# Chunkwise memory update: VectorE's work of a step in another order, with the pending result and its statistics moved into two waits

## The reference, cut to what matters

```python
def step(M, chunk):
    ...                                     # eta, alpha: means of sigmoids of the chunk
    outputs = einsum('bci,boi->bco', chunk, M)
    k_mean = (chunk / norm(chunk)).mean(axis=1)
    v_target = value_gen(outputs).mean(axis=1)   # value_gen(y) = silu(y @ w1.T) @ w2.T + y
    err = v_target - einsum('boi,bi->bo', M, k_mean)
    M_new = alpha * M + eta * err[:, :, None] * k_mean[:, None, :]
    M_new = gate * M_new + (1 - gate) * M
    M_norm = sqrt(sum(M_new * M_new))
    return M_new * minimum(30.0 / (M_norm + 1e-6), 1.0), outputs
M_final, outs = scan(step, M0, chunks)
x = x + value_gen(outs)
```

## Time and profile before

| | |
|---|---|
| median of 3 runs | 1940.58 us |
| lowest, highest run | 1935.58, 1942.81 us |
| profiled execution: span (no other time is listed for it) | 1946.8 us |
| TensorE busy over the span | 1855.2 us, 95% |
| VectorE busy over the span | 1348.6 us, 69% |
| ScalarE, GpSimd busy | 1179.6 us (61%), 416.6 us (21%) |
| the 16 memory steps | from about 66 to 228 us of the span |

### The profile page before, as it was taken

How to read it: one execution, slowest core, us unless ns; L and a number is a source line. 1 busy time by engine, 2 the same in 40 slices (tenths; PEclk the granted TensorE clock), 3 DMA queues, 4 the chain that set the end, 5 groups by cost and what they waited for, 6 DMA issues and landing times. The chain is left out here.

```text
span 1946.8 us, 51759 instructions
## 1 busy us (share of the span) xinstructions
PE 1855.2 (95%) x19836; PEld 1437.6 (74%) x19836; DVE 1348.6 (69%) x2724; ACT 1179.6 (61%) x2371; POOL 416.6 (21%) x497
## 2 busy tenths in 40 slices
PE   6998899999999888999999999999998999999998
PEld 5677789999999654465555555565545789999997
DVE  6555678544445877899999999999944877444445
ACT  5211354554545544799889988989895644445443
POOL 1121100455553333000000000000000002555541
PEclk9999999999999999999999999999999999999999
DMA  7000121222225665312122111111005211222228
GB/s 303 1 1 0 39 76 29 66 79 74 80 71 170 153 180 150 89 42 54 44 55 49 42 41 41 41 42 41 3 3 200 100 36 35 78 76 79 74 65 265
DMA packets 86539, 149.13 MB, mean 77 GB/s; under 512 B 35620, under 2 KB 69284, under 8 KB 80612
## 3 DMA queue, kind: packets, MB, share of 16 engines
q1 hardware_dynamic: 68428, 103.24, 17.6%
q0 software_dynamic: 17856, 42.60, 7.9%
q10 hardware_dynamic: 24, 0.02, 0.0%
HBM read 96.68 MB, written 48.76 MB: 75 GB/s over the span
## 5 line engine op out<-in xcount | busy, mean ns | idle before, releaser
L2201 ACT ACTIVATE att_scores_pt<-att_scores_psE 128x512 f32<-128x512 f32 x1024 | 598.1, 597 | 68.6 <-PE att_scores_psE L1705 26.3
L1720 DVE TENSOR_REDUCE att_mx<-att_scores_psS 128x1 f32<-128x1024 f32 x472 | 578.1, 1225 | 49.8 <-PE att_scores_psS L1705 18.5
L1705 PE MATMUL att_scores_psE<-att_qs,att_ks 99*32 99x512 bf16 x4096 | 438.1, 382 | 3.9 <-DVE att_scores_psO L2231 3.1
L2303 PE MATMUL att_scores_psO<-att_scores_pt,att_va 128*17 128x256 f32 x4096 | 330.5, 379 | 2.9 <-ACT att_scores_osb L2206 1.3
L1705 PE MATMUL att_scores_psS<-att_ks,att_qs 96*32 96x512 bf16 x3776 | 308.8, 380 | 0.1
L1705 PEld LDWEIGHTS att_scores_psE<-att_qs,att_ks 99*32 99x32 bf16 x4096 | 137.0, 95 | 102.8 <-ACT att_scores_pt L2201 8.8
L2303 PEld LDWEIGHTS att_scores_psO<-att_scores_pt,att_va 128*17 128x17 f32 x4096 | 132.5, 98 | 102.3 <-issue 13.2
L658 DVE TENSOR_TENSOR moe_hidT_rest<-moe_ps,moe_hidT_high 128x384 fp32r<-128x384 f32 x142 | 79.2, 558 | 184.9 <-ACT moe_hidT_high L377 172.2
L865 PE MATMUL moe_ps<-W_rest,moe_srcT_high 128*128 (+2 forms) x824 | 200.3, 324 | 0.0
L283 POOL DMA_INDIRECT expert_rows<-work,moe_slots_i x142 | 140.0, 986 | 218.8 <-issue 108.1
L1705 PEld LDWEIGHTS att_scores_psS<-att_ks,att_qs 96*32 96x32 bf16 x3776 | 127.1, 98 | 77.0 <-issue 1.3
(11 more groups left out here) (327 smaller groups left out, 3146.3 us busy)
## 6 DMA issues: line engine op xcount, KB each, us to landing
W_gate_up<-in_gate_up_dram SPq DMA_DIRECT2D x2, 6346.0 KB, 21.8
work<-expert_rows SPq DMA_DIRECT2D x12, 1024.0 KB, 7.9
query_key_parts<-att_qkv_parts SPq DMA_DIRECT2D x64, 192.0 KB, 2.8
normalised_rows<-work SPq DMA_DIRECT2D x64, 128.0 KB, 1.9
att_qs<-query_key_parts SPq DMA_DIRECT2D x16, 384.0 KB, 4.4
att_ks<-query_key_parts SPq DMA_DIRECT2D x16, 384.0 KB, 4.5
W_down<-in_down_a_dram SPq DMA_DIRECT2D x2, 2304.0 KB, 28.1
work<-normalised_rows SPq DMA_DIRECT2D x36, 128.0 KB, 2.1
```

What stands on the lines that cost most here:

```text
L1705: last = nc.tensor.matmul(out[j:j + 32, :], stationary[:, j:j + 32], moving, start=True, stop=True, tile_position=(0, j), skip_group_check ...
L1720: return nc.vector.tensor_reduce(a.mx[g % 2][:, v:v + 1], bank[:, :, :].rearrange("p h k -> p (h k)"), AX.X, ALU.max)
L2201: nc.scalar.activation(pt[s % 2][:, r, :], psE[use % E_BANKS][:, :], ACT.Exp, scale=HD ** -0.5).then_inc(p_ready, 1)
L2303: last = nc.tensor.matmul(psO[32 * r:32 * r + VC, cols], va[g][:, kt, r * VC:(r + 1) * VC], pt[s % 2][:, r, cols], start=(kt == 0 and part ...
```

## The change

VectorE's stream in the 16 steps is put in another order. Nothing is added or removed except that a result and its statistics are now carried into the next step; no other engine's stream is edited.

- `scaled` (the two L1378 products) is the first thing in a step.
- The second final result of the step in front (`left`) follows it.
- The reciprocal rA and n2's product (L1441, L1442) and their drain stand behind that, where they stood at the end of the step in front; rA now reads `scale`, which is the same tile.
- `ye`, f, n2c and cA come after these, behind `scaled` and ahead of the hidden sums, where they stood ahead of `scaled`.
- `statistics` of the step in front stand between the write of n2 and the wait for the root.

```diff
-            def step(tq, v, no_result, first=False, last_step=False):
+            def step(tq, v, no_result, first=False, last_step=False, left=None):
                 t = tq * 4 + v
                 q, c = v // 2, v % 2
                 scale = A[v % 2]
 
+                scaled(t, q, c, scale)
+                if left is not None:
+                    result(*left, 1)
+                if not first:
+                    nc.vector.reciprocal(rA[:, :], scale[:, :])
+                    nc.vector.tensor_tensor(n2[:, :], n2[:, :], scl[:, :], ALU.mult)
+                    dve.drain()
                 if last_step:
-                    scaled(t, q, c, scale)
+                    if left is not None:
+                        statistics(*left)
                     for i in range(2):
                         result(tq, v, i)
                     statistics(tq, v)
@@ (the new A unchanged) @@
                 dve.drain().then_inc(A_ready, 1)
-                nc.vector.reciprocal(rA[:, :], A[1 - v % 2][:, :])
-                nc.vector.tensor_tensor(n2[:, :], n2[:, :], scl[:, :], ALU.mult)
-                dve.drain()
-                if not no_result:
-                    result(tq, v, 1)
-                    statistics(tq, v)
@@ (the calls) @@
+            def step_in_front(tq, v):
+                return (tq, v - 1) if v else (tq - 1, 3)
+
             for v in range(4):
-                step(0, v, v < 2, v == 0)
+                step(0, v, v < 2, v == 0, left=(0, 2) if v == 3 else None)
             with dve.Fori(1, NC // 4 - 1) as tq:
                 for v in range(4):
-                    step(tq, v, False)
+                    step(tq, v, False, left=step_in_front(tq, v))
             for v in range(4):
                 ...
-                step(NC // 4 - 1, v, False, False, v == 3)
+                step(NC // 4 - 1, v, False, False, v == 3, step_in_front(NC // 4 - 1, v))
```

## The result

| | before | changed |
|---|---|---|
| median, 17 runs each | 1940.58 us | 1935.37 us |
| lowest to highest | 1934.81 to 1945.96 | 1929.05 to 1942.25 |
| ratio, 95% interval | | 0.9974 [0.9963, 0.9985] |
| profiled execution | span 1946.8 us | span 1931.2 us, time 1932.97 us |
| memory block, from the first L1572 (now L1578) to the end of the last result | 161.0 us | 155.9 us |

The change makes the kernel 0.26% faster, 5.0 us of 1940.6, and the block in which it stands is 5.1 us shorter (both block lengths are two starts of rows subtracted, plus the last row's length). The rest of the 15.6 us between the two spans lies in phases whose code is the same. The changed kernel profiled a second time had a span of 1944.1 us with a block of 156.0 us, so a span can't be used for a comparison of this size, and the block can.

The account below looks back on a forecast made before the run. VectorE's queue up to the hidden sums was taken to bound a step, TensorE next. Terms -7.4 + 1.9 + 0.8 = -4.7 us took the profiled 1946.8 to 1942.1; less 6.2 to the median, 1935.9 us (1932 to 1939).

Parts of the forecast that it names:

- the 0.1 for register work: Loop steps: of 0.27 us of issue before the result, 0.1 us taken on the path (bounds 0 and 0.27).
- Steps 3 to 14: TensorE's wait for VectorE's hidden sums falls from 10.5 us to 3.1 us over these steps: gain 7.4 us.
- The hold on n2's product: n2's product, due at 137.52, meets GpSimd's L1121 and is held until 137.69, 0.14 us before L1121's end.
- TensorE as next bound: TensorE lies 0.83 us behind VectorE's queue; after the change it is free at 139.05 in place of 138.90.
- Rival A: More comes back: n2's product slips past L1121, and the clock may add 1.6 us; time 1931.7 us, chance 0.20.
- idle 0.2 to 0.3 us: Sign of being right: TensorE's idle before L1587 at 0.2 to 0.3 us in steps 3 to 14.
- Statistics: A drain and two `bn_stats` hide in the 1.12 us wait for the root, 0.18 to spare; cost taken as 0.
- Steps 0 to 2: No result to move; small products come late and run into L1121: losses 0.58, 0.97 and 0.35, together 1.9 us.
- Step 15: The result in front starts only behind both scalings, so L1542 and TensorE's tail move later: loss 0.8 us.
- The clock: TensorE's clock changes, priced only in rivals: 1.6 us gained in Rival A, 9 us lost in Rival B.
- Rival B: Longer idle in steps 0 and 1 keeps TensorE at half speed through steps 1 and 2: 9 us, time 1944.9, chance 0.12.

Follow-up runs that it names:

- factors_first: Changed kernel with rA, n2's product and their drain ahead of the scaling: ratio 0.9950 to the kernel before, block 152.8 us, loop step 9.14 us.
- gps_half: Changed kernel with GpSimd's L1121 over half its elements, half the outputs left unscaled: ratio 0.9969 to the kernel before, block 151.8 us, loop step 9.24 us.
- stats_behind: Changed kernel with the statistics right behind the second result, out of the root's wait: ratio 1.0016 to the kernel before, block 163.4 us.
- early_old: Changed kernel with steps 0 to 2 alone in the order of the kernel before: ratio 0.9964 to the kernel before, block 152.6 us.
- result_first: Changed kernel with the second result ahead of the scaling: ratio 0.9968 to the kernel before, block 153.7 us, loop step 9.45 us.
- both_first: Changed kernel with result, rA, n2's product, drain ahead of scaling in steps 3 to 15, earlier steps as before: ratios 0.9941, 0.9963; blocks 149.4, 147.8 us.
- best_order: Changed kernel with steps 0 to 2 as before, factors ahead of scaling in steps 3 to 14, result ahead in step 15: ratio 0.9947, block 147.9 us.
- stats_only: Kernel before with only the statistics moved into the wait for the root: ratio 0.9979 to the kernel before, block 157.3 us, loop step 9.89 us.

## Why the prediction was right

The time was to be 1935.9 us (1932 to 1939) and is 1935.37. The mechanism held nearly to the hundredth: on the axis of the earlier trace rows (0.17 us taken off) the first scaling starts at 135.98 (135.95 predicted), the second at 136.74 (136.75), the result at 137.08 (137.09), n2's product at 137.50 (137.52), and L1593 at 139.18 (139.19 with the 0.1 for register work). The sum was less exact than its total looks:

- **Steps 3 to 14.** Predicted gain 7.4 us. They took 122.2 us and take 114.1, 8.1 less; 1.6 of these is the fall of the clock in step 12, which is gone, so the order's own gain is 6.5. A loop step was to take 9.4 to 9.5 us and takes 9.45. Of the 0.9 us that are missing, 0.65 lie in steps 5 and 14 (0.28 us gained in each, 0.6 predicted), where VectorE stands for 0.28 us in front of f and for 0.16 us in front of cA. Both are rows of "issue", whose source no run told apart.
- **The hold on n2's product.** Predicted release 0.14 us before L1121's end; measured 137.67 + 0.35 - 0.13 = 137.89 with L1121 ending at 138.00, so 0.11. From there to L1593 predicted 1.50 (with the 0.1 for register work), measured 1.46. Inside the term two sizes were off against each other: drain and register work took 0.20 in place of 0.35, and the products from `ye` to cA 0.46 in place of 0.35, as in the loop they start 0.11 us apart and not 0.07.
- **TensorE as next bound.** The prediction took TensorE as free at the modelled end of L1551 (138.90), and 0.15 us later with the bank's wait. By the rows of factors_first it is free 0.44 us behind L1551's start, not 0.61: at 138.74 in the kernel before, and 9.01 us after its last start; 9.23 in the changed kernel. So the bank costs 0.22 us in place of 0.15, and the wait before L1587 was 0.99 us and is 0.23, which the weight loads show (1.02 and 0.25) and the matmul rows don't (0.83 and 0.06). The gain of a step hung on VectorE and didn't suffer. Rival A's price did: it gave 0.14 us for a loop step without the hold, and gps_half won 0.21. The sign "idle 0.2 to 0.3 us" was reckoned against the old free time, too; by the prediction's own 139.05 the matmul rows had to show 0.04 to 0.14 (they show 0.00 to 0.06 in nine of the twelve steps).
- **Statistics.** Taken at 0; the root's distance is unchanged and stats_behind gives the price of the other place, 0.72 us a step.
- **Steps 0 to 2.** Predicted loss 0.58 in step 0: 4.98 - 4.40 = 0.58. Predicted 0.97 + 0.35 in steps 1 and 2: the time from error 0 to error 2 grew by 1.63 us in place of 1.32. From L1121 to L1593 it is 2.30 us in both steps, just as predicted (82.52 - 80.22, 90.37 - 88.07). But the row compared with was taken while TensorE came late from 1.2 GHz: at full clock the old order of step 1 has 1.57 us there (early_old, 76.95 to 78.52) and not 1.33, so that its loss is 0.73. Where the clock falls alike, once and in step 1, the new order takes 19.0 us from error 0 to error 2 (stats_behind, result_first) and the old one 18.0 to 18.1 (early_old, both_first, best_order): a loss of 0.9 to 1.0 us. The rest of the 1.63 is then the clock's.
- **Step 15.** Predicted 0.8; the tail grew by 0.75 us.
- **The clock** was left out of the sum and priced in two rivals. The fall in step 12 went (rival A's 1.6 us). Rival B's further time at 1.2 GHz didn't come: the changed kernel's clock falls twice in steps 0 and 1 where the kernel before had one longer stretch, and the mean over the first 26 us is 0.87 in both, by these windows of before and changed:

```profile
66.00:92.00 26.00, 23.81 (x108) 19.32 (x107) 11.60 (x65) 5.38 (x14) 5.18 (x5) 0.87 0.00 1
66.00:92.00 26.00, 21.95 (x96) 17.60 (x94) 11.98 (x60) 5.38 (x14) 5.19 (x5) 0.87 0.00 0
```

So -4.7 us became -5.1 in the block partly by luck: -6.5 + 0.58 + 1.63 + 0.75 is -3.5 us, and the fall of the clock in step 12 that went adds 1.6, which the sum hadn't counted. That the time came out within 0.6 us of the forecast is luck as well, as the interval of the ratio alone spans 2 us either way.

What remains open is what makes TensorE's clock fall. It was not tried to fill the idle stretches with other matmuls.

## What to carry to other kernels

When an engine's queue is reordered to take work off a path, the instructions that used to be free in a wait must land in another wait: list the waits with their lengths, and put each instruction where a wait of its length stands (statistics 0.93 us in the root's 1.12; factors 0.4 in the first layer's 0.45). Check each small instruction for what it runs beside: here one product of 128x4 elements cost up to 1.03 us because GpSimd was at work, and moving others ahead of it gained nothing. A wait that comes out shorter than its price may be hidden by a modelled end: read the weight load beside the matmul. For a change of 5 us under a run-to-run spread of 10, compare the length of the changed block in the profiles, with the granted clock in it, and look at the time of the phase behind it before you count the block's gain as the program's.

## What the runs showed of the hardware

- A VectorE product with two inputs in SBUF that is issued while GpSimd's two-input product runs ends 0.01 to 0.03 us behind it, however early it started: 128x4 products that take 0.13 to 0.15 us alone took from 0.18 to 1.03 us (n2's product and f, over all runs). Exempt are those of the first and the last moment: one that started 0.07 us ahead of GpSimd's wasn't held (cA in step 3 of stats_only, 0.15 us), and one that started within its last 0.1 us took its own 0.15. Products with one input in PSUM, reciprocals, reductions and `bn_stats` beside it kept their lengths.
- Idle time of TensorE doesn't tell whether its clock falls: 1.27 us was followed by a fall in the kernel before, 1.33 us not; 0.90 us in stats_behind was followed by one in step 4 and not in step 8; 0.87 us was followed by one in both_first and 0.86, in the same order and step, not.
- Register work of the loop shows where it can't run ahead. Behind a drain an instruction whose wait and addresses are ready starts 0.07 us after it, but the result in the loop 0.20 to 0.33 us, 0.44 us at the start of the loop's first trip and 0.79 us at the start of its second (both_first, result_first). Behind a long instruction the same work cost nothing (the result behind the scaling, 137.25 - 136.91 = 0.34 us, as in the written-out steps).
- A matmul row can show no wait where the engine did wait: TensorE took up L1593 0.44 us behind L1557's start when nothing was waited for, where the modelled end says 0.61.
